# Last stage of a graph kernel: two accumulator sets by turns, and pairs of edge tiles addressed by register

## What is computed

```python
# three stages; src, dst: the two ends of the 100000 edges, sorted by dst
h = relu(layernorm(x))
x = x + gcn_two_layers(h, src, dst)          # each: segment_sum(norm * (h @ W)[src], dst) + dense terms
h = relu(layernorm(x))
x0, x1 = lin_irreps(h)                       # "up" projection, 128 + 3*128 features per node
w1, w2, w3, w4 = split(mlp(edge_attr_8))     # radial network, 512 weights per edge
s0, s1, y0, y1 = x0[src], x1[src], edge_attr_4[:, 0:1], edge_attr_4[:, 1:4]
m0 = concat([w1*s0*y0, w4*sum(s1*y1, -1)/sqrt3])
m1 = concat([(w2*s0)[:,:,None]*y1[:,None,:], w3[:,:,None]*s1*y0[:,None,:]])
x = x + lin_irreps(segment_sum(m0, dst), segment_sum(m1, dst)) / 10
```

## Time and profile before

| what | value |
|---|---|
| median of 3 runs | 5402.21 us (5398.03 to 5405.94) |
| the profiled execution | 5398.43 us, span 5396.6 us |
| PE, DVE, ACT, POOL busy | 88%, 52%, 41%, 50% of the span |
| GCN layer 0, layer 1, last stage | about 541 to 1793, 1850 to 3073 and 3108 to 5389 us |
| DMA, mean | 171 GB/s |

### The profile page before, as it was taken

The page is one execution under the profiler, slowest core; times in us unless marked ns, Lnnn a source line. Parts: engine busy times, 40 slices in busy tenths (PEclk is TensorE's granted clock), DMA queues, the critical chain, the costliest instruction groups (busy, mean ns, idle before and its releaser), DMA issues.

```text
span 5396.6 us, 99589 instructions
## 1 busy us (share of the span) xinstructions
PE 4750.2 (88%) x15182; PEld 2032.8 (38%) x15183; DVE 2801.5 (52%) x6919; ACT 2239.5 (41%) x6181; POOL 2719.5 (50%) x3416
## 2 busy tenths in 40 slices
PE   7899887778889888677788789999999999999999
PEld 5344222223344323233344433333333344444443
DVE  7543012233445201223344467777777777777776
ACT  0443222111223222111222366666666666666665
POOL 0332666666666466676666444444444444334332
PEclk9999898888999898788898999999999999999999
DMA  2232776667778677777788744444444444444443
GB/s 84 92 109 96 213 215 201 212 215 234 236 237 260 188 216 216 214 223 246 247 259 265 225 126 126 124 122 128 124 129 128 125 125 126 128 125 125 129 127 107
DMA packets 434963, 921.11 MB, mean 171 GB/s; under 512 B 63349, under 2 KB 171125, under 8 KB 434790
## 3 DMA queue, kind: packets, MB, share of 16 engines
q0 software_dynamic: 197120, 646.08, 40.8%
q1 hardware_dynamic: 182918, 245.65, 13.4%
q10 hardware_dynamic: 54880, 28.91, 1.8%
HBM read 791.98 MB, written 128.41 MB: 171 GB/s over the span
## 4 chain that ended last, share of the span: by engine, by line
PE 62%; issue 12%; DVE 8%; another core or an unknown queue 7%; DVEq 5%; DMA 3%; ACT 1%; ACTq 1%; POOL 0%; SPq 0%; POOLq 0%
PE bank L1415 21%; PE bank L1289 12%; PE bank L1405 6%; PE bank L1244 3%; PE bank L1246 3%; PE bank L1334 3%; PE bank L1336 2%; DVE dense_w L1140 2%; DMA ef<-in_ef_t_dram 2%; PE bank L1268 1%; PE bank L1350 1%; DVE hA L1131 1%; PE bank L1438 1%; PE bank L1280 1%
## 5 line engine op out<-in xcount | busy, mean ns | idle before, releaser
L547 POOL DMA_INDIRECT ring<-tab_d,idx x1584 | 1566.1, 989 | 785.8 <-issue 471.8
L1289 PE MATMUL bank<-ring,ohp 128*128 x3904 | 1073.8, 423 | 348.5 <-issue 259.6
L796 ACT ACTIVATE dense_w<-hA,hC 128x128 f32<-128x128 f32 x2640 | 819.3, 389 | 703.7 <-DVE hA L1127 519.7
L514 POOL DMA_INDIRECT ring<-up_d,idx x880 | 855.2, 972 | 501.8 <-POOL idx L510 352.4
L1415 PE MATMUL bank<-dense_w,yb 128*128 128x512 f32 x1760 | 934.6, 613 | 1.5 <-DVE dense_w L1144 1.5
L1415 PE MATMUL bank<-dense_w,oh 128*128 128x512 f32 x1760 | 898.7, 592 | 0.0
L1289 PEld LDWEIGHTS bank<-ring,ohp 128*128 x3904 | 401.8, 104 | 997.5 <-issue 706.0
L1035 DVE TENSOR_TENSOR ohp<-iota_w,dst_f 128x512 f32 x392 | 268.2, 693 | 761.1 <-remote 259.6
L510 POOL COPY idx<-src_i 128x2 int32 x440 | 80.8, 184 | 860.8 <-DVE dense_w L1144 813.8
L1405 PE MATMUL bank<-w,hC 64*128 64x512 f32 x1760 | 498.3, 643 | 11.6 <-DMA hC<-hid_d 11.6
L1415 PEld LDWEIGHTS bank<-dense_w,oh 128*128 128x128 f32 x1760 | 334.4, 190 | 420.9 <-issue 420.9
(11 more groups left out here) (190 smaller groups left out, 5308.1 us busy)
## 6 DMA issues: line engine op xcount, KB each, us to landing
hC<-hid_d SPq DMA_DIRECT2D x440, 64.0 KB
ring<-tab_d,idx POOLq DMA_INDIRECT x1584
tab_d<-tout SPq DMA_DIRECT2D x98, 256.0 KB, 2.7
tw<-tab_d SPq DMA_DIRECT2D x98, 256.0 KB
hlw<-hl_d SPq DMA_DIRECT2D x98, 256.0 KB
hid_d<-hC ACTq DMA_DIRECT2D x98, 256.0 KB
hl_d<-agg SPq DMA_DIRECT2D x74, 256.0 KB, 3.0
ring<-up_d,idx POOLq DMA_INDIRECT x880
```

What stands on the lines that cost most here:

```text
L514: g_.indirect_dma_start(ring_v[:, b, k, :], None, table, bass.IndirectOffsetOnAxis(idx_t[:, b, k:k + 1], 0)).then_inc(S["got"][b], 16)
L547: g_.indirect_dma_start(ring_h[:, slot, k, :], None, table, bass.IndirectOffsetOnAxis(idx_b[:, slot, k:k + 1], 0)).then_inc(S["got"][slot] ...
L796: ac.mul(msg[:, b, k, 1, P + m * P:2 * P + m * P], t2[:, b, k, :], yg[:, b, 4 * k + 1 + m:4 * k + 2 + m])
L1289: ins = pe.matmul(bank[0][:, :], ohp_b[:, bass.ds(at, 1), k, :].rearrange("p b n -> p (b n)"), ring_b[:, bass.ds(slot, 1), k, h, :].rearra ...
```

## The change

Two sets of accumulators are used by turns: banks 0 and 1 for even windows, 6 and 7 for odd ones. While one set adds up a window, the other is copied out, takes the transposes, and then the output product. The first matmul of a window starts its bank, so the `touch` matmuls go. The copies come after the second pair of the next window, the transposes behind PE's second pair, the copy of the turned sums and the output product behind the fourth; `MINV` goes from 4 to 7. PE's window loop holds two windows (`over_sets`). POOL now waits itself for the landing of the gather before and raises one semaphore, `arrived`, for which ACT and DVE wait; they address the gathered slot by register and choose by branches only between two buffers. The diff, cut to its core (the DVE part of what is shown for ACT alone has the same form):

```diff
-MINV = 4
+MINV = 7
...
+        def over_sets(eng, window):
+
+            window(0, 0)
+            with eng.Fori(0, NW // 2 - 1) as j:
+                window(j * 2 + 1, 1)
+                window(j * 2 + 2, 0)
+            window(NW - 2, 1)
+            window(NW - 1, 0)
...
+        def sums(w, h):
+
+            if isinstance(w, int):
+                return ps[:, 6 * (w % 2) + h, :]
+            return ps[:, bass.ds(w % 2 * 6 + h, 1), :].rearrange("p b n -> p (b n)")
...
+                        landed = g_.snap((n + (buffers - 1 - LAG)) // buffers * 32)
...
                             for k in range(2):
                                 g_.indirect_dma_start(ring_v[:, b, k, :], None, table,
                                                       bass.IndirectOffsetOnAxis(idx_t[:, b, k:k + 1], 0)).then_inc(S["got"][b], 16)
+                            with g_.If(n > LAG):
+                                g_.wait_ge(S["got"][(b - LAG) % buffers], landed)
+                                g_.nop().then_inc(S["arrived"], 1)
                         pick(g_, g_.snap(n % buffers), 0, buffers, gather)
                 peeled(g_, [(0, body)])
+                total = g_.snap(c)
+                for b in range(buffers):
+                    g_.wait_ge(S["got"][b], g_.snap((total - 1 + (buffers - b) % buffers) // buffers * 32))
+                g_.nop().then_inc(S["arrived"], LAG)
...
-                def pair(u):
-                    b = u % 2
+                u = ring_u[:, bass.ds(ac.snap(n % NU), 1), :, :].rearrange("p b k n -> p (b k) n")
+
+                def pair(b):
...
-                    ac.wait_ge(M["got"][u], ac.snap((n + (NU - 1)) // NU * 32))
+                    ac.wait_ge(M["arrived"], n)
...
-                pick(ac, ac.snap(n % NU), 0, NU, pair)
+                pick(ac, ac.snap(n % 2), 0, 2, pair)
...
+            def keep_a(w, behind=0):
+                ac.wait_ge(M["seg_done"], ac.snap(c) + (1 - behind))
+                after(ac, M["turned"], w)
+                ac.copy(mA[:, :], sums(w, 0)).then_inc(M["mA"], 1)
+
+            def copy_mT(w):
+                times = ac.snap(turned_r)
+                after(ac, M["o_done"], w)
+                ac.wait_ge(M["turned"], times)
+                ac.reg_add(turned_r, turned_r, 1)
+                ac.copy(mT[:, 0:4, :], sums(w, 0).rearrange("p (c n) -> p c n", c=4)).then_inc(M["mT_a"], 1)
+
+            def window(w):
+
+                lo, hi = ac.snap(lo_r), ac.snap(hi_r)
+                if not isinstance(w, int) or w > 0:
+                    with ac.Fori(lo, lo + 2) as g:
+                        weigh(g)
+                    keep_a(w - 1, 2)
+                    with ac.Fori(lo + 2, lo + 4) as g:
+                        weigh(g)
+                    copy_mT(w - 1)
+                    lo = ac.snap(lo + 4)
+                if not isinstance(w, int) or w < NW - 1:
+                    next_range(w + 1)
+                with ac.Fori(lo, hi) as g:
                     weigh(g)
 
...
-                def pair(ub):
-                    b, u = ub % 2, ring_u[:, ub, :, :]
+                u = ring_u[:, bass.ds(ve.snap(n % NU), 1), :, :].rearrange("p b k n -> p (b k) n")
+
+                def pair(b):
...
-                    ve.wait_ge(M["got"][ub], ve.snap((n + (NU - 1)) // NU * 32))
+                    ve.wait_ge(M["arrived"], n)
...
                 ve.drain()
                 ve.tensor_scalar(iota_w[:, :], iota_w[:, :], float(P), None, ALU.add)
                 if not isinstance(w, int) or w > 0:
                     finish(w - 1)
...
+            def sum_pair(n, b, p, first):
-                        ins = pe.matmul(bank[h][:, :], (oh0, oh)[h][:, b, k, :], msg[:, b, k, h, :], start=False,
-                                        stop=(last and k == 1), skip_group_check=True)
+                        ins = pe.matmul(sums(p, h), (oh0, oh)[h][:, b, k, :], msg[:, b, k, h, :], start=(first and k == 0),
+                                        stop=False, skip_group_check=True)
...
+            def window(w, p):
                 lo, hi = window_range(pe, w)
-                after(pe, M["mA"], w)
-                after(pe, M["mB"], w)
-                touch(bank[0][:, :], D, True)
-                touch(bank[1][:, :], D, True)
+                if not isinstance(w, int) or w > 1:
+                    pe.wait_ge(M["out_ready"], w - 1)
+                step(p, first=True)
+                step(p)
                 if not isinstance(w, int) or w > 0:
-                    turn_m(w - 1)
-                step(True)
+                    turn_m(w - 1, 1 - p)
+                with pe.Fori(lo + 2, lo + 4) as g:
+                    step(p)
+                if not isinstance(w, int) or w > 0:
+                    out_product(w - 1, 1 - p)
                 if not isinstance(w, int) or w < NW - 1:
-                    step(True)
-                    if not isinstance(w, int) or w > 0:
-                        out_product(w - 1)
-                    with pe.Fori(lo + 2, hi - 1) as g:
-                        step(True)
-                    step(True, True)
+                    with pe.Fori(lo + 4, hi) as g:
+                        step(p)
                 else:
-                    with pe.Fori(lo + 1, hi - 2) as g:
-                        step(True)
-                    out_product(w - 1)
-                    step(False)
-                    step(False, True)
+                    with pe.Fori(lo + 4, hi - 2) as g:
+                        step(p)
+                    step(p, ahead=False)
+                    step(p, ahead=False)
...
-            over_windows(pe, window)
+            over_sets(pe, window)
```

More of the change, by code:

```diff
@@ L305, in over_windows @@
             window(0)
-            window(1)
-            with eng.Fori(2, NW - 1) as w:
+            with eng.Fori(1, NW - 1) as w:
                 window(w)
             window(NW - 1)
+        def over_sets(eng, window):
[5 more added lines that the diff above has]
+            window(NW - 1, 0)
         block = ctx.enter_context(nc.Block())
@@ L807, in first_pair @@
                 ac.reg_mov(hi_r, hi)
-                weigh(lo)
-            def second_pair(w):
-                weigh(ac.snap(lo_r) + 1)
-            def rest(w):
-                with ac.Fori(ac.snap(lo_r) + 2, ac.snap(hi_r)) as g:
-                    weigh(g)
-            def keep_a(w):
-                more = 1 if isinstance(w, int) and w == NW - 1 else 0
-                ac.wait_ge(M["seg_done"], ac.snap(c) + more)
-                after(ac, M["turned"], w)
-                ac.copy(mA[:, :], bank[0][:, :]).then_inc(M["mA"], 1)
@@ L823, in copy_mT @@
-            def copy_mT(w):
-                ac.wait_ge(M["turned"], w + 1)
-                after(ac, M["o_done"], w)
-                ac.copy(mT[:, 0:4, :], m_bank[0][:, :].rearrange("p (c n) -> p c n", c=4)).then_inc(M["mT_a"], 1)
-            def window(w):
-                second_pair(w)
-                if not isinstance(w, int) or w > 0:
-                    copy_mT(w - 1)
-                rest(w)
-                if not isinstance(w, int) or w < NW - 1:
-                    first_pair(w + 1)
-                keep_a(w)
@@ L1145, in pair, with next_range @@
                     ve.reg_add(c, c, 1)
[L1146 to L1148 removed]
+                pick(ve, ve.snap(n % 2), 0, 2, pair)
+            def next_range(w):
                 lo, hi = window_range(ve, w)
@@ L1151, in first_pair, with keep_b @@
                 ve.reg_mov(hi_r, hi)
-                messages(lo)
-            def second_pair(w):
-                messages(ve.snap(lo_r) + 1)
-            def rest(w):
-                with ve.Fori(ve.snap(lo_r) + 2, ve.snap(hi_r)) as g:
-                    messages(g)
-                ve.drain()
-                ve.tensor_scalar(iota_w[:, :], iota_w[:, :], float(P), None, ALU.add)
-                ve.drain()
-            def keep_b(w):
-                more = 1 if isinstance(w, int) and w == NW - 1 else 0
-                ve.wait_ge(M["seg_done"], ve.snap(c) + more)
+            def keep_b(w, behind=0):
+                ve.wait_ge(M["seg_done"], ve.snap(c) + (1 - behind))
                 after(ve, M["turned"], w)
-                ve.tensor_copy(mB[:, :], bank[1][:, :]).then_inc(M["mB"], 1)
+                ve.tensor_copy(mB[:, :], sums(w, 1)).then_inc(M["mB"], 1)
             def copy_mT(w):
-                ve.wait_ge(M["turned"], w + 1)
+                times = ve.snap(turned_r)
                 after(ve, M["o_done"], w)
-                ve.tensor_copy(mT[:, 4:8, :], m_bank[1][:, :].rearrange("p (c n) -> p c n", c=4)).then_inc(M["mT_b"], 1)
+                ve.wait_ge(M["turned"], times)
+                ve.reg_add(turned_r, turned_r, 1)
+                ve.tensor_copy(mT[:, 4:8, :], sums(w, 1).rearrange("p (c n) -> p c n", c=4)).then_inc(M["mT_b"], 1)
             def finish(w):
@@ L1179, in finish @@
                 after(ve, M["stored"], w, 16)
[L1180 removed]
```

(25 more changed lines are left out.)

41 lines of the change are left out of this document (13 added, 28 removed).

## The result

| | before | after | forecast |
|---|---|---|---|
| median of the runs | 5404.07 us | 5928.51 us (four runs, 5918.34 to 5934.50) | 5858 us (5785 to 5920) |
| ratio, 95% interval | 1 | 1.0966 (1.0944 to 1.0989) | 1.084 |
| profiled execution, its span | 5398.4, 5396.6 us | 5934.4, 5932.6 us | 5853.9 us |
| pairs of the last stage | 440 | 473 | 473 |
| transfers of the layers' gathers | 1584 | 1872 | 1872 |

The change makes the kernel 9.7% slower. That is 8.5 us beyond the upper end of the range and 70.5 us above the number.

A forecast was written before the change was run, and what follows sets the result against it. It took PE to bound the last stage and mostly the gathers to bound the layers. From the profiled 5398.4 us, + 154.8 + 357.7 - 57 gave 5853.9, and 3.8 us for the median made 5858 us, range 5785 to 5920.

The forecast's parts named there:

- Counts: Last stage and layers' gathers: index copies rise from 440 to 473, gather transfers from 1584 to 1872.
- Pairs of the last stage: Last stage: at least seven pairs a window adds 33 pairs of 4.69 us each, +154.8 us.
- The layers: Last 24 windows of each layer: 88 blocks instead of 55, at 6.21 and 6.07 us a block, +357.7 us.
- Rival 1: Layers' late windows: gathers speed up to 263 GB/s, +242 us in place of +358, total 5742 us; chance 0.09.
- Window ends: Last stage: zero matmuls and copy waits go, -68.6 us; DVE's lateness of 0.25 us a window returns +12; sum -57 us.
- Rival 3: Last stage: DVE becomes the bound through exposed register work, 30 to 60 us more, total 5890 to 5920 us; chance 0.06.
- Moved copies: Last stage: DVE's and ACT's copies after the second pair delay nobody, 0; at most 0.8 to 0.9 us a window.
- slots by register: DVE's pair code: between 0.2 us less and 0.56 us more a pair, hidden by DVE's idle time, taken as 0.
- `arrived`: POOL's new wait for landings and the later signal to DVE and ACT cost 0, also at the last stage's start.
- fetches: PE's loop of two windows: no repeated instruction fetches, 0; bound from above 2.3 us a window.
- Rivals 2 and 4: No padding, only window ends change, 5345 us (0.03); PE's double loop fetched again each round, 106 us more, 5964 us (0.02).

The follow-up runs named there:

- e1: The kernel before the change with only MINV raised from 4 to 7: 5925.48 us, ratio 1.0976 to the kernel before.
- e2: The changed kernel with MINV back at 4, PE's last window rewritten to suffice with five pairs: 5396.75 us, ratio 0.9986 to the kernel before.
- e3: Against e2, ACT and DVE choose among four slots by branches with fixed addresses instead of by register: 5415.63 us, ratio 1.0017 to the kernel before.
- e8: Against e7, the one-hots' base has two buffers chosen by register, so its update and drains leave the window's end: 5187.10 us, ratio 0.9945 to the kernel before.
- e6: Against e2, PE makes the output product after the third pair instead of the fourth: 5214.37 us, ratio 1.0001 to the kernel before on the same chip.
- e7: Against e2, output product after the third pair and DVE's residual after the fifth: 5181.26 us, ratio 0.9935 to the kernel before on the same chip.

## Why the prediction came out too low

**The direction and the mechanism were right.** Slower, through the padding, which is not in the change's title. e1 shows it by itself: +522 us with one constant, where I had 154.8 + 357.7 = 512.5.

**Counts.** 473 pairs and 1872 transfers, as worked out.

**Pairs of the last stage.** 33 x 4.69. The pair is still 3.63 + 1.06 us. e1's stage is 157.0 us longer than before (forecast 154.8).

**The layers.** Forecast +357.7; measured +376.5 in the changed kernel and +346 in e1. The code of the layers is the same in both, and the forecast lies between the two. That their difference is the scatter of single executions is not shown: at four pairs the same stretches of the kernel before, e2 and e3 agree within 4.3 and 3.0 us. By the medians, all that comes ahead of the last stage grew by 524.4 - 148.4 = 376 us in the changed kernel and by 522.2 - 157.0 = 365 us in e1, so this part of the forecast was 7 to 18 us too low. I had said 6.1 to 6.2 us a block; it was 6.36 and 6.18 after, 6.13 and 6.10 in e1 (352 and 347 transfers). Rival 1, gathers at 263 GB/s, is out: 220 and 239.

**Window ends: the step that failed.** The part about what goes was right to a tenth. Before, a window end cost 2.33 us over 48 windows (I took 2.3 from two of them): 0.43 zero matmuls, 1.03 waiting, 0.87 transposes. What stays was nearly right too, 0.93 for the transposes where I had 0.87. The failed step is "Between nothing and twice today's lateness, I take 0.25 us". DVE's lateness is 1.24 us a window, five times that and beyond the bound. The term should have been 2.33 - 0.93 - 1.24 = 0.16 us a window, 8 us and not 57. This is 49 of the 80.5 us between the forecast for a profiled execution (5853.9) and the one seen (5934.4); the layers' late windows are 19, their early ones 6 or 7, the break before the last stage 5. By itself the failed step would have left the forecast at 5858 + 49 = 5907 us, inside the range; together with what the layers took more it came out beyond the upper end.

Where the lateness comes from, at the edge shown above. Before, the sums would have been 0.3 us late even without a copy. Ahead of the lines of the earlier trace rows DVE ended the old window with these:

```profile
3507.18 0.42 DVE L1144 TENSOR_TENSOR dense_w<-hB,bank 128x256 f32<-128x256 f32 x1
3507.71 0.23 DVE L1161 TENSOR_SCALAR iota_w<-iota_w 128x128 f32<-128x128 f32 x1
```

I put the new drain and loop start off against the range reading that leaves. They don't cancel: from the base's step to the next one-hot are 2.48 us here (2.15 in the mean before), so 0.33 us more. DVE's pair grew by 0.08 us (3.39 instead of 3.31 from the one-hot to the last instruction; by the medians of the stage to its end, 3.83 instead of 3.77). And DVE comes to the edge 0.28 us later relative to PE (its last instruction starts 0.26 us ahead of PE's next weights, 5475.64 against 5475.90, where it was 0.54). Together that is 1.0 us for the 0.95 seen. The other 0.29 us is the second pair, which I hadn't looked at: before, PE lost 2.33 us at each edge, and DVE's second round was hidden behind that; now its 4.98 us lie bare as well. That the parts add up so is arithmetic on the trace; of them, only the register addressing was taken away by itself (e3), and the base with its drain (e8).

A second error stood behind it. I compared DVE with PE at an edge where PE was late, and called the steady state covered: DVE's 1.0 us a pair ahead of its one-hots hides register work within a window, but across an edge DVE has the residual, the base and the loop on top. From L1144 to L1144 that was 6.01 us before (3507.18 to the 3513.19 of the earlier trace rows), 1.3 us over PE's 4.69. This surplus was always there, and PE's old 2.3 us at the edge paid for it.

**Rival 3, DVE becomes the bound.** Right in its place (the window's start) and in size (30 to 60 us; it was 49), wrong in its cause: I gave it register work, and e3 shows that branches cost as much. It had 6 chances in 100, though the earlier trace rows showed DVE late at just that place, and the upper end of 5920 took in only "some of rival 3".

**Moved copies, slots by register, `arrived`, fetches.** All taken as 0. The copies: transposes and product start 1.06 us after their weights, with no idle time. `arrived` is used in the last stage alone; what queues behind its wait on POOL, the index copy L525, waits for DVE in 828.0 of its 854.5 idle us. It was not tried by itself. Fetches: 13 and 25 packets, not one for each round of a loop; this agrees with my reading of the Trainium skill ("Runtime: NRT & Kernel Launch", section "Instruction fetch mechanics"), by whose room for 2048 instructions the double loop fits. The rule itself is stated there for a window of two pages, at 256 instructions a page; my estimate of 700 or 800 instructions would not fit into that, and the packets speak against this reading. Rivals 2 and 4 are out by the counts and the packets.

**What stays open.** How the 1.24 us divide between drain, loop start, branches and the longer pair, as only two of these were taken away. And why e3 is 19 us above e2 where their last stages differ by 9: the layers, whose code is the same, took the rest in its profile. And why the layers' late stretches are 31 us longer in the changed kernel's profile than in e1's.

## What to carry to other kernels

Read what a constant is used for outside of the stage that the change names: here a minimum run length set the gathers of two other stages, and the kernel lost 522 us by it, where the rearranged accumulators alone brought 6.6 us that cannot be told from nothing. When a stall of the bounding engine is removed, add up the follower's whole round across that point (here 6.4 us against 4.69), since the old stall paid for it, and look one round further too. To free a window's edge, move work so that both sides of its dependence move: the residual alone made it slower, the product alone did nothing, both together gave 0.65%.

## What I had not expected of the hardware

- Two chips differ by 3.6% on the same kernel (5403.33 and 5210.72 us), and it is mostly the layers that differ: from the end of their first window to that of their last are 2332 us in e2 and 2168 us in e6. In order, the late stretches of the layers in e2 on the first chip, the gathers alone, and then those of e7 on the second:

```profile
1430.00:1786.00 356.00, 219.31 (x216) 0.98 0.81 249
2707.00:3071.00 364.00, 216.13 (x218) 0.92 0.82 262
```

```profile
1346.00:1679.00 333.00, 227.93 (x224) 0.99 0.84 269
2549.00:2895.00 346.00, 218.14 (x221) 0.94 0.83 273
```

  The same gathers run at 269 and 273 GB/s instead of 249 and 262, while the last stage, which PE bounds, takes the same time to within 0.4% (2255.9 in e2, 2263.4 in e6, whose waits are 11 us longer in sum). I haven't found why.
- Work that is not counted as busy adds up at an edge: in the 1.35 us from the residual's end to the next one-hot the longest pieces are 0.28 us of "issue" and 0.14, 0.10 and 0.24 us for the loops and the address. The drain's 0.60 us ahead of them run beside the residual.
- With the padding PE's granted clock, here a mean over stretches at both of its levels (1.0, 2.4 GHz, and 0.5, 1.2 GHz), fell in the late windows of layer 0 from 0.97 to 0.90, PE being busy 80% of the time instead of 93%; e1 shows the same, 0.89.
